# The MLP's first norm moved to TensorE in a four-layer kernel

## The reference, cut to what matters

```python
# g = group norm of x over the image, without weight
mu = jnp.mean(x2, axis=-1, keepdims=True)               # x2: tokens of g, 64 channels each
var = jnp.mean(jnp.square(x2 - mu), axis=-1, keepdims=True)
h = (x2 - mu) * jax.lax.rsqrt(var + eps) * ln_w + ln_b
scale = jnp.clip(jnp.max(jnp.abs(h), -1, keepdims=True), 1e-12, None) / 448
hq = (h / scale).astype(float8_e4m3fn)                  # row by row; w1 and w2 likewise
ab = (hq @ w1q.T) * scale * sw1.T                       # 512 wide: a, b
out = quantised(relu(a) * b) @ w2q.T ...
```

## Time and profile before

| | |
|---|---|
| time, median of 3 runs | 1909.69 us (1905.93 to 1915.94) |
| profiled execution, its own time | 1910.86 us |
| its span, first to last instruction | 1909.1 us |
| DVE busy in the span | 1604.4 us, 84% |
| PE busy | 1332.1 us, 70% |
| ACT busy | 1152.5 us, 60% |
| POOL busy | 1056.8 us, 55% |
| mean granted clock of TensorE | 0.853 of full speed |
| first pipeline of layer 2 | about 905 us to 1146 us |

### The profile page before, as it was taken

One profiled execution on the slowest core, in us unless ns is written; L12 is line 12 of the kernel. 1 busy time (PEld: TensorE's weight loads), 2 busy tenths in 40 slices (PEclk: granted clock), 3 DMA queues, 4 the chain that ended last, 5 costly groups with the idle time before them and its releaser, 6 DMA issues.

```text
span 1909.1 us, 29191 instructions
## 1 busy us (share of the span) xinstructions
PE 1332.1 (70%) x8880; PEld 884.1 (46%) x8880; DVE 1604.4 (84%) x3965; ACT 1152.5 (60%) x2464; POOL 1056.8 (55%) x730
## 2 busy tenths in 40 slices
PE   5579998799699988997000005667666669998765
PEld 1146667665366667664000002333333337777654
DVE  6899981698799943997999998999999879992488
ACT  2246661699365632996444447777777537772498
POOL 7288850487688801775867650333333478870254
PEclk8779999899899989899555555898989789999789
DMA  6034435487344443776222211444444624435377
GB/s 245 0 86 106 108 77 145 121 227 212 92 105 106 96 120 86 201 197 174 66 61 63 58 39 28 103 100 109 111 100 100 134 82 111 111 89 140 106 257 249
DMA packets 408828, 225.43 MB, mean 118 GB/s; under 512 B 343456, under 2 KB 343776, under 8 KB 408672
## 3 DMA queue, kind: packets, MB, share of 16 engines
q1 hardware_dynamic: 270240, 185.81, 35.7%
q10 hardware_dynamic: 138432, 37.76, 8.5%
HBM read 114.97 MB, written 66.06 MB: 95 GB/s over the span
## 4 chain that ended last, share of the span: by engine, by line
issue 33%; PE 28%; DVE 15%; ACT 10%; POOL 8%; DMA 4%; SPq 0%; ACTq 0%; DVEq 0%; POOLq 0%
PE ps L1085 10%; ACT work L945 7%; PE ps L1090 7%; PE ps L1046 4%; POOL work L503 4%; PE ps L1075 4%; PE ps L1165 3%; DMA gate_dram<-work 3%; POOL work L457 3%; DVE stats L683 2%; ACT work L931 2%; DVE ln_s L699 1%; DVE work L710 1%; DVE work L604 1%; DVE pairs L801 1%
## 5 line engine op out<-in xcount | busy, mean ns | idle before, releaser
L497 POOL TENSOR_TENSOR ln_s<-ln_s,half_power 128x8 f32<-128x8 f32 x252 | 418.8, 1662 | 366.7 <-DVE ln_s L692 315.4
L1046 PE MATMUL ps<-work,ones 128*128 128x512 f32 x504 | 283.0, 678 | 56.5 <-ACT work L907 46.2
L1085 PE MATMUL ps<-work 128*128 128x384 f32 x864 | 318.8, 492 | 2.1 <-ACT work L931 2.1
L1179 PE MATMUL ps<-w1s,pairs 64*128 64x256 bf16 (+1 forms) x864 | 105.7, 362 | 280.4 <-DMA pairs<-pairs 240.8
L956 ACT ACTIVATE work<-ps 128x768 f32<-128x768 f32 x216 | 175.4, 812 | 170.8 <-DMA gate_dram<-work 136.8
L945 ACT ACTIVATE work<-pairs,ln_s 128x64 f32<-128x64 f32 x648 | 262.7, 490 | 17.7 <-DVE ln_s L699 17.7
L503 POOL TENSOR_TENSOR work<-pairs,work 128x512 f32<-128x512 f32 x36 | 75.9, 2109 | 270.4 <-DVE pairs L864 270.4
L1090 PE MATMUL ps<-work 128*128 128x256 f32 x864 | 222.8, 380 | 0.0
L489 POOL TENSOR_TENSOR work<-work,gn_rstd 128x512 f32<-128x512 f32 x144 | 185.0, 1286 | 62.4 <-DVE work L648 56.9
L1179 PEld LDWEIGHTS ps<-w1s,pairs 64*128 64x128 bf16 x864 | 34.2, 103 | 373.8 <-issue 273.3
L1090 PEld LDWEIGHTS ps<-work 128*128 128x128 f32 x864 | 165.4, 191 | 69.7 <-issue 1.8
(11 more groups left out here) (125 smaller groups left out, 2761.7 us busy)
## 6 DMA issues: line engine op xcount, KB each, us to landing
work<-x_mid SPq DMA_DIRECT2D x144, 256.0 KB, 2.9
gate_dram<-work ACTq DMA_DIRECT2D x108, 256.0 KB, 3.1
work<-gate_dram SPq DMA_DIRECT2D x108, 256.0 KB, 3.4
work<-in_x_in SPq DMA_DIRECT2D x72, 256.0 KB, 2.8
work<-x_nat SPq DMA_DIRECT2D x144, 128.0 KB, 3.1
x_mid<-work SPq DMA_DIRECT2D x72, 256.0 KB, 2.6
work<-pairs SPq DMA_DIRECT2D x96, 96.0 KB, 3.0
work<-pairs ACTq DMA_DIRECT2D x96, 96.0 KB, 3.1
```

The source lines that it names most:

```text
L497: pool.tensor_tensor(ln_s[:, b, RSTD, :], ln_s[:, b, VAR, :], half_power[:, 0:U], ALU.pow)\
L1046: last = pe.matmul(ps[:, bank, :], ones[:], src[:, b, :], start=first, stop=end, skip_group_check=True)
L1085: last = pe.matmul(ps[:, GATE_BANK[half] + k, 0:GATES], xnT[:, b, (2 * half + k) * P:(2 * half + k + 1) * P], wpair[:, VALUES:VALUES + GAT ...
```

## The change

In layer 2's first pipeline the norm is done by PE, ACT and fewer steps on DVE:

- PE turns the raw tile x (`turn_x`, four transposes): channels now lie on partitions, so the group norm is a scale and a bias per partition. ACT applies both while it moves the tile from PSUM to SBUF (`evacuate_channels`, into `x_chan`, a ring of four).
- PE multiplies by `w_centre` (identity minus 1/64, `centred`, four matmuls of 128 columns), which subtracts each token's mean and turns the tile back: the result, in PSUM with tokens on partitions, serves only for the variance (DVE `h_moments`, `h_var`).
- POOL makes the token's deviation sigma with one power of 1/2 (`h_sigma`); PE turns it (`turn_sigma`), ACT moves it to SBUF (`evacuate_sigma`, 128x128).
- PE multiplies `x_chan` by `w_centre_scale` (centring and weight in one, `weighted`, four matmuls of 128 columns) and adds sigma times the bias by one matmul of 512 columns (`biased`). So the bank holds h times sigma. Since the rounding divides each row by its largest magnitude, sigma cancels; only the squares of the scales are divided by the variance, once for all tiles (`squares_of_scales`).
- `centre` and `normalise` in layer 2, `h_weight`, `h_bias`, POOL's `scale` and the copy of the scales are gone. `h_amax` and `h_rescale` read PSUM now.
- POOL builds the matrices once (`mlp_weights`), ahead of `group_rstd(2)`, in room of `work` that layer 1's output pipeline used: it waits for the last `project_out`. DVE, PE and DVE make the two columns of scale and bias (`gn_pair`, `gn_column`).

```diff
-                    pipeline(pool, [(4, lambda t, b, r: scale(l, t, b, r), RING),
-                                    (3, lambda t, b: token_rstd(l, 0, t, b)),
-                                    (1, h_bias)])
+                    pipeline(pool, [(2, h_sigma)])
...
+            def mlp_weights():
+                pool.wait_ge(out_ready, 2 * TILES)
+                pool.memset(work[:, 3072:3072 + 2 * P], 0.0).then_inc(h_weights, 1)
+                pool.tensor_tensor(tokens(w_bias), over_tokens(mlp_wb[:, 1, :]), over_channels(ident[:, 0:U]), ALU.mult)                    .then_inc(h_weights, 1)
+                pool.memset(w_centre, 0.0).then_inc(h_weights, 1)
...
+            def h_sigma(t, b):
+                pool.wait_ge(h_var_ready, t + 1)
+                wait_free(pool, sigma_turned, t - 1)
+                wait_free(pool, h_step, 4 * (t - 2) + 2)
+                pool.tensor_tensor(sigma[:, b, 0:U], var_all[:, t, :], root_power[:], ALU.pow).then_inc(sigma_ready, 1)
...
+            def h_moments(t, b):
+                dve.wait_ge(centred_ready, t + 1)
+                for k in range(PAIRS):
+                    last = dve.bn_stats(stats[:, b, k, :],
+                                        ps[:, CENTRED_BANK + b, 2 * k * C:(2 * k + 2) * C].rearrange("p (e c) -> p c e", e=2))
+                last.then_inc(h_moments_ready, 1)
...
+            def h_clip(t, b):
+                dve.wait_ge(h_step, 4 * t + 1)
+                dve.scalar_tensor_tensor(out=tok[:, 1, :], in0=sigma[:, b, 0:U], scalar=1e-12, in1=tok[:, 0, :],
+                                         op0=ALU.mult, op1=ALU.max).then_inc(h_step, 1)
...
             def h_rescale(t, b):
-                dve.wait_ge(h_step, 3 * t + 3)
-
-                dve.tensor_tensor(tokens(h_scaled[:, b, :]), tokens(h_act[:, b, :]), over_channels(tok[:, 2, :]), ALU.mult)\
+                dve.wait_ge(h_step, 4 * t + 4)
+                dve.tensor_tensor(tokens(h_scaled[:, b, :]), tokens(ps[:, H_BANK + b, :]), over_channels(tok[:, 2, :]), ALU.mult)\
                     .then_inc(hs_ready, 1)
...
-                    pipeline(dve, layer_norm(l, 0, h_norm, 2, [(0, h_amax), (0, h_scale)]) + [
-                                   (1, h_weight),
-                                   (0, h_inverse),
-                                   (-1, h_add),
-                                   (0, h_rescale),
-                                   (-1, h_round),
-                                   (5, lambda t, b, r: centre(l, t, b, r), RING)])
+                    pipeline(dve, [(0, h_amax), (2, h_moments),
+                                   (0, h_clip), (2, h_var),
+                                   (0, h_scale), (-1, h_add), (0, h_inverse), (-1, h_round), (0, h_rescale)])
+                    squares_of_scales()
...
+            def evacuate_channels(t, b, r):
+                if t == 0:
+                    act.wait_ge(column_ready, 1)
+                act.wait_ge(x_turned, t + 1)
+                wait_free(act, g_ready, t - 3)
+                act.activation(x_chan[:, r, :], ps[:, T_BANK + b, :], ACT.Identity, scale=gn_column[:, 0:1], bias=gn_column[:, 1:2])\
+                    .then_inc(x_chan_ready, 1)
+
+            def evacuate_sigma(t, b):
+                act.wait_ge(sigma_turned, t + 1)
+                wait_free(act, g_ready, t - 1)
+                act.activation(sigma_row[:, b, :], ps[:, SIGMA_BANK, 0:P], ACT.Copy).then_inc(sigma_row_ready, 1)
...
-                    pipeline(act, [(2, lambda t, b, r: normalise(l, 0, h_norm, lambda t: wait_free(act, hw_ready, t - 1), t, b, r), RING),
-                                   (0, h_abs)])
+                    pipeline(act, [(-1, h_abs), (4, evacuate_channels, RING), (1, evacuate_sigma)])
...
+            def turn_x(t, b):
+                pe.wait_ge(x_loaded[b], tile_landed(X_LOADS, 2, t, b))
+                wait_free(pe, x_chan_ready, t - 1)
+                for k in range(PAIRS):
+                    last = pe.transpose(ps[:, T_BANK + b, k * P:(k + 1) * P], xin[:, b, k * P:(k + 1) * P], ident[:])
+                last.then_inc(x_turned, 1)
+
+            def centred(t, b, r):
+                pe.wait_ge(x_chan_ready, t + 1)
+                wait_free(pe, h_moments_ready, t - 1)
+                for k in range(PAIRS):
+                    last = pe.matmul(ps[:, CENTRED_BANK + b, k * P:(k + 1) * P], x_chan[:, r, k * P:(k + 1) * P], w_centre,
+                                     start=True, stop=True)
+                last.then_inc(centred_ready, 1)
+
+            def turn_sigma(t, b):
+                pe.wait_ge(sigma_ready, t + 1)
+                wait_free(pe, sigma_row_ready, t)
+                pe.transpose(ps[:, SIGMA_BANK, 0:P], sigma[:, b, :], ident[:]).then_inc(sigma_turned, 1)
+
+            def weighted(t, b, r):
+                wait_free(pe, hs_ready, t - 1)
+                for k in range(PAIRS):
+                    pe.matmul(ps[:, H_BANK + b, k * P:(k + 1) * P], x_chan[:, r, k * P:(k + 1) * P], w_centre_scale,
+                              start=k == 0, stop=False, skip_group_check=True)
+
+            def biased(t, b):
+                pe.wait_ge(sigma_row_ready, t + 1)
+                pe.matmul(ps[:, H_BANK + b, :], sigma_row[:, b, :], w_bias, start=False, stop=True, skip_group_check=True)\
+                    .then_inc(g_ready, 1)
...
+                    pipeline(pe, [(4, turn_x), (3, centred, RING), (1, turn_sigma), (1, weighted, RING), (1, biased)])
```

More of the change, by code:

```diff
@@ L145, in build @@
         wide = pairs[:].rearrange("p a c n -> p (a c n)")
-        h_norm, h_pre, h_act, h_scaled, h_added = (part(wide, 1024 * k, ROW) for k in range(5))
+        h_scaled, h_added = (part(wide, 1024 * k, ROW) for k in range(2))
         h_magic = part(wide, 5120, ROW // 2).bitcast(BF16)
@@ L155, in build @@
         q_hidT = part(work, 2048, U * HID // 2).bitcast(BF16).rearrange("p b (k n) -> p b k n", n=P)
+        x_chan = part(work, 1024, ROW, RING)
+        sigma, sigma_row = (part(work, 3072 + 2 * P * k, P) for k in range(2))
+        w_centre, w_centre_scale = (work[:, 3584 + P * k:3584 + P * (k + 1)] for k in range(2))
+        w_bias = work[:, 3840:3840 + ROW]
+        gn_pair = work[:, 4352:4352 + 4 * C].rearrange("p (k e c) -> p k e c", k=2, e=2)
         xres_m, prod_m = part(work, 8192, ROW), part(wide, 17408 + TILES * ROW, ROW)
@@ L164, in build @@
         half_power = sb("half_power", [P, U])
+        root_power = sb("root_power", [P, U])
+        gn_column = sb("gn_column", [P, 2])
         wfold = sb("wfold", [P, 3, PROJ + C])
@@ L235, in build @@
          mlp_out_ready, mres_loaded,
-         s_apart) = [sem(f"sem_{k}") for k in range(69)]
+         s_apart) = [sem(f"sem_{k}") for k in range(81)]
         x_loaded, gate_stored, xnew_stored, mres_loaded, qT_ready, hqT_ready = [
@@ L507, in shift_new @@
                 shift(xnew[:, b, :], sum_base(l) + t, b)
[L509 to L513, removed]
+            def mlp_weights():
[3 more added lines that the diff above has]
+                pool.memset(w_centre, 0.0).then_inc(h_weights, 1)
+                for e in range(2):
+                    rows = slice(C * e, C * e + C)
+                    pool.wait_ge(h_weights, 3 + e)
+                    pool.tensor_scalar(w_centre[rows, rows], ident[rows, rows], 1.0 / C, None, ALU.subtract).then_inc(h_weights, 1)
+                pool.wait_ge(h_weights, 5)
+                pool.tensor_tensor(w_centre_scale.rearrange("p (e c) -> p e c", e=2), w_centre.rearrange("p (e c) -> p e c", e=2),
+                                   mlp_wb[:, 0, :].unsqueeze(1).to_broadcast([P, 2, C]), ALU.mult).then_inc(h_weights, 1)
+            def h_sigma(t, b):
[3 more added lines that the diff above has]
+                pool.tensor_tensor(sigma[:, b, 0:U], var_all[:, t, :], root_power[:], ALU.pow).then_inc(sigma_ready, 1)
             for l in range(layers):
+                if l not in TRIANGLES:
+                    mlp_weights()
                 group_rstd(l)
@@ L772, in h_amax, with h_var @@
+            def h_var(t, b):
+                dve.wait_ge(h_moments_ready, t + 1)
+                dve.tensor_scalar(var_all[:, t, :], of_stats(b, 2), C * LN_EPS, None, ALU.add).then_inc(h_var_ready, 1)
             def h_amax(t, b):
[L773 to L774 removed]
+                dve.wait_ge(g_ready, t + 1)
+                dve.tensor_reduce(tok[:, 0, :], tokens(ps[:, H_BANK + b, :]), AX.X, ALU.max, apply_absolute_value=True)\
@@ L1210, in _ @@
                 else:
+                    pe.wait_ge(h_weights, 6)
+                    pe.wait_ge(gn_doubled, 2)
+                    for k in range(2):
+                        last = pe.matmul(ps[:, COLUMN_BANK, k:k + 1], gn_pair[:, k, :, :].rearrange("p e c -> p (e c)"), ident[:, 0:1],
+                                         start=True, stop=True)
+                    last.then_inc(column_spread, 1)
+                    pipeline(pe, [(4, turn_x), (3, centred, RING), (1, turn_sigma), (1, weighted, RING), (1, biased)])
```

79 lines of the change are left out of this document (46 added, 33 removed).

## The result

The changed kernel takes 1814.81 us, median of 4 runs (1812.79 to 1818.28), against 1910.06 us (1905.93 to 1915.94, 4 runs) before: ratio 0.9494, 95% interval 0.9471 to 0.9516. The forecast was 1819 us. The profiled execution took 1815.44 us with a span of 1813.7 us.

The account below looks back on a forecast made before the run. DVE, with stalls caused by POOL, bounds layer 2's first pipeline. Its period falls from 6.55 to 3.70 us, the next pipeline's first matmul comes 91.7 us earlier: 1910.86 - 91.7 = 1819 us; range 1804 to 1860.

Parts of the forecast that it names:

- What bound the kernel before: Layer 2's first pipeline: DVE sets the 6.55 us period, including POOL-caused stalls of 1.07 (`h_rescale`) and 0.5 us (`ln_shift`).
- Rival 3: `h_rescale`'s stall stays: period 4.8 to 5.2 us, time 1858 to 1870; chance 0.09 shared with half clock for part.
- DVE's work per tile: DVE's remaining instructions in layer 2's first pipeline: 3.64 us from rows, forecast 3.70, bounds 3.45 to 4.05.
- an allowance for PSUM: 0.06 us a tile added for six DVE instructions that change their source from SBUF to PSUM.
- PE below DVE: PE's transposes and matmuls take 3.2 us a tile at full clock, below DVE's 3.70.
- Rival 1: Hand-offs, not DVE, set the period at full clock: 4.1 to 4.8 us, time 1833 to 1858; chance 0.18.
- the way (a): Wait path from `h_rescale(t-2)` through ACT's `h_abs` and two evacuations to `biased(t)`: 3.3 us of the 3.70 available.
- (b): Wait path from `h_var(t)` through POOL's power, transposing, ACT and `biased`: 5.8 us of two periods, 7.4.
- The half clock of the start: PE starts the pipeline at clock 0.50 after idling; first `h_amax` at 917, bounds 914 and 921.
- Rival 2: PE stays at 1.2 GHz: period 6.7 us, time 1928 us, slower by 0.9%; chance in full 0.04.
- The sum: 917 + 35 x 3.70 = 1046.5, then 2.14 and 5.34: next pipeline's first matmul at 1054.0, 91.7 us earlier.
- my own range: Total time 1807 to 1833 us for DVE at 3.45 to 4.05 us a tile; chance 0.66.

Follow-up runs that it names:

- runs 1: Kernel before, with POOL's bias addition (`h_bias`) narrowed to one token of eight: 1883.04 us, ratio 0.9834.
- run 2: Kernel before, with both whole-tile POOL instructions of layer 2 (`scale` and `h_bias`) narrowed to one token of eight: 1867.87 us, ratio 0.9755.
- run 4: Changed kernel with one of the four moment instructions per tile: 1803.19 us, ratio 0.9417 to the kernel before.
- run 3: Changed kernel with each centring matmul issued twice: 1837.43 us, ratio 0.9596 to the kernel before.
- run 7: Changed kernel with `h_rescale` issued five times a tile: 1900.37 us, ratio 0.9919 to the kernel before.
- run 5: Changed kernel with an added 128x512 POOL addition a tile behind POOL's power: 1812.64 us, ratio 0.9462 to the kernel before.
- run 6: Changed kernel with an added 128x512 POOL addition a tile ahead of POOL's power: 1840.87 us, ratio 0.961 to the kernel before.

## Why the prediction was right

**What bound the kernel before.** Right, and shown. Each piece of the 6.55 us that I took for a stall went when POOL's instruction was narrowed: the period fell by 0.95 of the 1.07 put down to `h_rescale` and by 0.46 of the 0.5 put down to `ln_shift` (runs 1, 2). Rival 3, a stall that stays, is refuted.

**DVE's work per tile.** I had 3.64 from rows and 3.70 with an allowance for PSUM. Measured is 3.60. The three small ones took 0.27 (0.30 forecast), `h_amax` and `h_rescale` 0.60 each (0.61), the moments 0.80 (0.79). The allowance was the part that was too large: a moment instruction has a mean of 283 ns from PSUM against 275 from SBUF before, `h_amax` 681 against 673, `h_rescale` 683 against its undisturbed 679. The 65 ns for each of these that the Trainium skill's figures would give (VectorE: DVE Perf Modes, the section on the TRN2 errata) do not appear; the same section says of its SBUF figure that it is too low. The tile's 0.10 is the largest term of the miss, 35 x 0.10 = 3.5 us.

**PE below DVE.** Right: 3.2 us a tile from layer 0's rows, 3.20 measured when DVE was made faster (run 4), 4.08 when 0.89 was added (run 3). Rival 1 is refuted by the same two runs, and by the 0.85 us between the end of `biased` and `h_amax`. In the way (a) two of my prices were off in opposite senses: ACT's evacuation with scale and bias takes 0.76 us, not 0.63, and the one of sigma 0.27, not 0.63. In (b) the power takes 2.08 and not 1.67. Neither way came near to deciding.

**The clock.** The half clock of the start was there, and gone sooner than I allowed: full from about 910 us on. So the first `h_amax` came at 915.38 and not at 917. Rival 2 did not happen. At 5.99 us a tile (run 7) the clock falls for short stretches and recovers each time while the pipeline is in its steady state. What a kernel would look like in which the half clock holds itself in this pipeline was not found.

**The sum.** First `h_amax` 1.6 us early; 35 periods at an average 3.57 (the last ones lack the moments) 124.9 us, not 129.5; from there to the last `h_rescale` 2.33, not 2.14; to the first matmul 5.43, not 5.34. Together the matmul is at 1048.0, not at 1054.0. Of these 6 us, 2.3 are lost again in the 766 us behind it, less than that unchanged stretch varies (763.1 to 771.2 us). So that the time came within 4 us of the forecast is in part luck: the stretch that was forecast came out 6 us early. The upper end of my own range was added up wrongly: 4.05 us a tile and a first `h_amax` at 921 give 1835 us, not 1833. `mlp_weights` was through at 898.7, 2.9 us before the power behind it, and `squares_of_scales` ended at 1047.75, 0.3 us before the first matmul, as counted on; its reciprocal of 288 elements takes 1.95 us.

**Where the 95 us came from.** Per period 1.41 us were POOL's whole-tile instructions holding DVE, 1.54 us DVE's own instructions and the 0.13 that the narrow addition still cost (runs 1, 2 against the changed kernel). Times 36 that is 51 and 55 us, 106 in all. It is less because the first period and the last four of the kernel before took 4.5 to 5.5 us each, so that its mean period was 6.29 and not 6.55: 35 x (6.29 - 3.57) = 95.2. With the first `h_amax` 3.0 us earlier and the end 0.8 us longer, the first matmul of the next pipeline is 97.7 us earlier, of which run 2 alone has 51.5, and the profiled time 95.4 us shorter.

## What to carry to other kernels

When DVE is busy all the time, compare each instruction's duration in the steady stretch with its duration where POOL is idle. The difference is not work, and it can be had back by giving POOL less to do, by giving DVE an operand in PSUM, or by moving the POOL instruction beside a DVE instruction with at most one input in SBUF. Read the granted clock in slices of one or two microseconds before saying that it held: a mean of 0.91 was full clock with stretches at half. An idle PE can take over elementwise work with a matrix form, if its sum, priced from the same batches elsewhere in the trace at both clocks, stays below that of the engine it relieves.

## What the runs showed of the hardware

- The same POOL addition (128x512 f32, both inputs in SBUF) cost DVE nothing beside instructions that read one tile from PSUM (run 5), and 0.72 us a tile beside `h_round`, with two inputs in SBUF (run 6). In the kernel before, DVE's product of PSUM and SBUF (L755, at most 0.69 us in 108) and the moments from one tile in SBUF (0.87 for four) were not lengthened beside such an instruction either.
- It works the other way too. POOL's power on 128x8 lasted 2.08 us where it started 0.1 us into `h_add`, and 1.64 us where no such instruction ran (917.39 in the changed kernel's timeline). In the kernel before it took 1.65 us though `h_weight`, with two inputs in SBUF, ran from 0.7 us behind its start, and `h_weight` kept its 0.68 too: not the whole of the power is in conflict with DVE.
- With PE busy for two thirds of the time in bursts of some 4 us in every 6, the granted clock fell to half for some 3.5 us nine times in 190 us and came back to full each time. The mean, 0.91 to 0.94, shows neither level.
